# Copying the second half of the sums behind the third of four Silu passes in a fused decoder kernel

## What is computed

```python
q = (X @ W_Q + b_Q).reshape(Bv, Tv, H_TOT, DH).transpose(0, 2, 1, 3)   # 64 heads of 16
k = jnp.tile(k_base, (1, N_BR, 1, 1)); v = jnp.tile(v_base, (1, N_BR, 1, 1))
q, k = (_rope(q), _rope(k))
scores = jnp.einsum('bhtd,bhsd->bhts', q, k) * ATTNSCALE
w = jax.nn.softplus(scores / jnp.sqrt(key_self)[:, :, None, :])
w = jnp.where(causal, w, 0.0)
w = w * jax.nn.sigmoid(SCALE * w)                    # Silu, up to a factor
w = jnp.where(w < sinks, 0.0, w)                     # threshold
total = jnp.sum(w, axis=-1, keepdims=True) + sinks + 1e-06
out = jnp.einsum('bhts,bhsd->bhtd', w / total, v)    # the sums
out = out + probs_sink * v_null
y = jnp.einsum('bntc,ncd->bntd', context, W_O) + W_O_bias[None, :, None, :]
return y.mean(axis=1)
```

## Time and profile before

| | us |
|---|---|
| median of 3 runs | 3050.16 |
| lowest and highest run | 3041.3, 3050.38 |
| the profiled execution | 3048.71 |
| its span, first to last instruction | 3046.9 |
| PE busy in the span | 2660.8 (87%) |
| DVE busy | 1783.8 (59%) |
| ACT busy | 1558.1 (51%) |
| POOL busy | 801.1 (26%) |
| mean granted TensorE clock, share of full speed | 0.936 |

### The profile page before, as it was taken

The page is one execution under the profiler, slowest core; times in us unless marked ns, Lnnn a source line. Parts: engine busy times, 40 slices in busy tenths (PEclk is TensorE's granted clock), DMA queues, the critical chain, the costliest instruction groups (busy, mean ns, idle before and its releaser), DMA issues. The chain is left out here.

```text
span 3046.9 us, 49262 instructions
## 1 busy us (share of the span) xinstructions
PE 2660.8 (87%) x18536; PEld 2093.0 (69%) x18536; DVE 1783.8 (59%) x4040; ACT 1558.1 (51%) x3054; POOL 801.1 (26%) x889
## 2 busy tenths in 40 slices
PE   5888888888877689999979999999969999849998
PEld 4555555555545456777758888898967777748887
DVE  3565556546537656555646767666765555554444
ACT  2766566666545344444436656655546656542221
POOL 1222222222210144444432111111006666600000
PEclk8899899989879899999999999999989999979999
DMA  3000000000002211111110000000010000020000
GB/s 111 5 4 5 1 4 5 4 1 4 1 1 64 80 26 25 26 41 33 22 35 13 6 6 6 3 1 1 1 68 8 8 5 5 1 97 8 8 4 32
DMA packets 88763, 59.42 MB, mean 20 GB/s; under 512 B 55120, under 2 KB 78416, under 8 KB 88016
## 3 DMA queue, kind: packets, MB, share of 16 engines
q1 hardware_dynamic: 88528, 56.25, 6.2%
HBM read 39.46 MB, written 8.39 MB: 16 GB/s over the span
## 5 line engine op out<-in xcount | busy, mean ns | idle before, releaser
L682 DVE SCALAR_TENSOR_TENSOR a_w<-a_w,a_sinks 128x384 f32<-128x384 f32 x512 | 348.5, 734 | 79.2 <-ACT a_w L510 78.9
L2031 POOL TENSOR_SCALAR x_weights<-x_weights,x_sums 128x256 f32<-128x256 f32 x256 | 232.5, 928 | 272.4 <-DVE x_sums L2090 272.4
L1121 POOL TENSOR_SCALAR f_weights<-f_weights,f_sums 128x256 f32<-128x256 f32 x256 | 232.7, 928 | 271.2 <-DVE f_sums L1351 271.2
L491 ACT ACTIVATE a_w<-psum 128x1024 f32<-128x1024 f32 x192 | 187.2, 1029 | 207.6 <-PE psum L343 207.6
L338 PE MATMUL psum<-a_qT,a_kT_half 32*128 32x512 f32 x768 | 221.6, 658 | 6.9 <-ACT a_w L491 4.1
L1279 ACT ACTIVATE f_weights<-psum,f_negmax 128x256 f32<-128x256 f32 x256 | 118.0, 473 | 212.8 <-DVE f_negmax L1345 212.8
L343 PE MATMUL psum<-a_future,a_unit 32*128 32x128 f32 (+5 forms) x1536 | 218.2, 406 | 0.0
L1616 ACT ACTIVATE a_turned_w_hi<-psum 128x512 fp32r<-128x512 f32 x256 | 139.1, 596 | 142.5 <-PE psum L1526 142.5
L2001 ACT ACTIVATE x_weights<-x_masked_s,x_negmax 128x256 f32<-128x256 f32 x256 | 127.0, 497 | 137.2 <-DVE x_negmax L2082 137.2
L343 PEld LDWEIGHTS psum<-a_future,a_unit 32*128 32x128 f32 x1536 | 124.5, 197 | 97.8 <-issue 96.7
L1733 DVE TENSOR_REDUCE a_negmax<-psum 128x1 f32<-128x1024 f32 x128 | 156.6, 1224 | 55.7 <-PE psum L119 51.5
(11 more groups left out here) (357 smaller groups left out, 7395.7 us busy)
## 6 DMA issues: line engine op xcount, KB each, us to landing
f_xnT<-all_xnT_all SPq DMA_DIRECT2D x16, 256.0 KB, 2.3
f_pv_rows<-f_pv SPq DMA_DIRECT2D x8, 512.0 KB, 3.2
f_pv_groups<-f_pv_rows SPq DMA_DIRECT2D x8, 512.0 KB
f_w<-in_f_w SPq DMA_DIRECT2D x2, 2048.0 KB, 10.2
all_x_all<-in_x SPq DMA_DIRECT2D x1, 2048.0 KB, 8.5
a_xnT<-all_xnT_all SPq DMA_DIRECT2D x8, 256.0 KB, 2.3
x_xnT<-all_xnT_all SPq DMA_DIRECT2D x8, 256.0 KB, 2.3
x_ctxT<-in_x_ctxT SPq DMA_DIRECT2D x8, 256.0 KB, 2.9
```

The lines of the kernel that those rows point to most:

```text
L491: act.activation(to, of, ACT.Softplus).then_inc(plus_done, 1)
L682: ins = dve.scalar_tensor_tensor(part, part, sinks[:, col:col + 1], part, ALU.is_ge, ALU.mult)
L1121: ins = pool.tensor_scalar(w, w, sums[:, k, h, t:t + 1], None, ALU.mult)
L2031: ins = pool.tensor_scalar(w, w, sums[:, k, h, t:t + 1], None, ALU.mult)
```

## The change

In steps in which a quad has Silu passes, ACT's copy of the second half of the sums moves from behind the fourth Silu pass and the table loads (in step 4 also Ln and Exp) to a place between the third and the fourth Silu pass. In the steps without Silu passes the copy stays where it is. Its wait on `summed` and its signal `sums_taken` go with it.

```diff
@@ -508,6 +508,8 @@
                                     for h in range(2):
                                         wu = w[:, (2 * n + pair) % PAIR_RING, h].rearrange("p r t -> p (r t)")
                                         act.activation(wu, wu, ACT.Silu, scale=SILU_SCALE).then_inc(silu_done, 1)
+                                        if (pair, h) == (1, 0):
+                                            take_sums(sums_quad, 1, spare_bank(b, step, "sum", 1))
                             if ahead and step == 4:
 
                                 act.preload_act_table_set("natural_log_exp_and_others")
@@ -518,7 +520,8 @@
                                    .then_inc(knorm_ready, 1)
                             if quad or ahead and step == 4:
                                 act.preload_act_table_set("softplus")
-                            take_sums(sums_quad, 1, spare_bank(b, step, "sum", 1))
+                            if not quad:
+                                take_sums(sums_quad, 1, spare_bank(b, step, "sum", 1))
```

## The result

| | before | after | predicted |
|---|---|---|---|
| median, us | 3050.27 | 2974.01 | 2921 (2905 to 2960) |
| profiled execution, us (span) | 3048.71 (3046.9) | 2978.33 (2976.5) | |
| mean granted clock | 0.936 | 0.933 | |
| one full batch, us | 105.79 | 92.44 | 86.6 |

The ratio of after to before is 0.9754, 95% interval 0.9718 to 0.9791: faster by 2.5%, a little over half of what was forecast, and 14 us above the range. The direction and the cause of the stalls were right. The time that is missing went into TensorE's clock, at a place that the prediction named and took for unlikely.

What follows compares the result with a forecast made beforehand. TensorE was taken as the bound, stalled in even steps by ACT's late copy of the sums. Gains of 40.6 + 14.4 + 41.3 + 30.6 + 0.3 = 127.2 us took 3048.7 to 2921, range 2905 to 2960.

Steps and rivals of the forecast that it cites:

- What bounds the kernel, and why the copy came late: First self attention: TensorE sets the pace, idle 15.6 us a batch, waiting for ACT's copy behind four Silus and a load.
- No load for the copy: On ACT, the copy between Silus needs no table load; the rival with two loads, 2968, had 1 in 100.
- Step 0: Projections: stall shrinks by 2.7 us, 1.0 stays; full clock gains another 3.0; 5.8 a time, seven times, 40.6.
- Step 2: Window of step 2: the whole 2.40 us stall goes, no clock to be won; six times, 14.4.
- Step 4: Window of step 4: the 4.62 us stall goes, a new softplus stall of 1.4 appears; gain 5.9, seven times, 41.3.
- the new softplus stall lowers the clock: Rival, step 4: light work behind the new stall runs at half clock, losing up to 9.6 us; 2988, 5 in 100.
- Step 6: Output product: stall shrinks by 2.7 us, 2.0 stays; full clock gains another 2.4; 5.1 a time, six times, 30.6.
- the first rival: Clock still falls in the stalls left in steps 0 and 6; 35.4 us not won, 2957; 10 in 100.
- First and last batch: First batch: step 4's 5.9 us counted; last batch: step 0's 5.8 counted, its later steps nearly cancel, +0.3.
- The sum: Whole kernel: 40.6 + 14.4 + 41.3 + 30.6 + 0.3 = 127.2 us saved.
- The range: Whole kernel: 2906 to 2940 us for the forecast itself, 2905 to 2960 with most of the first rival.
- The second rival: Step 4: the new softplus stall lowers the clock, up to 9.6 us lost seven times, 67; 2988, 5 in 100.

Runs made afterwards that it cites:

- ln6_wait: Changed kernel with step 4's Ln, Exp and their load moved to step 6, plus two idle table loads ahead of step 4's softplus; 2966.5 us, ratio 0.9732.
- half2: Changed kernel with four more dense matmuls (0.86 us) in step 4's window, leaving part of the softplus wait; about 2961 us, ratio 0.9718.
- only4: Kernel before the change with the copy moved in step 4 alone, steps 0, 2 and 6 as before; 3053.3 us, ratio 1.0013.

## Why the prediction was wrong, by its own steps

- **What bounds the kernel, and why the copy came late.** Right. The stalls that it forecast, 1.0 in step 0, none in steps 2 and 4, 2.0 in step 6 and 1.4 for softplus, measured 0.93, none, 1.90 and 1.59 in the batch shown.
- **No load for the copy.** Right, as the earlier trace rows had it: the copy stands between the Silus with no load beside it. The Trainium skill's dearer switch with a drain ("ScalarE: Activation LUTs", "What ACT_TABLE_LOAD costs") is not to be seen after the change either: the fourth Silu ends at 380.92, the load starts at 380.94 and Ln at 382.23.
- **Step 0.** Right to 0.1 us, clock and DVE chain included: 2.9 + 2.8 against 5.8.
- **Step 2.** Right, 2.6 against 2.4.
- **Step 4.** The term itself is right, 5.9, and the next late wait was named. The step that failed is what it leaves behind: the prediction let the 20 us behind the new stall run at full clock and gave "the new softplus stall lowers the clock" 5 in 100. It happened in all seven batches (0.55 to 0.63 over the 14 us behind the wait), and cost 4.5 us in the batch shown. Its argument against was that dense projections come straight before; the changed kernel and ln6_wait show that they don't protect the stretch. A nearer row was on the table: the earlier trace rows hold a stall of 2.40 without a fall, but with projections behind it, and a stretch at 0.50 in the last batch, which stands behind a stall of the same length with light work behind it. The prediction reasoned from the first of these. PE in the kernel before, ahead of the stretch from 814.80:

```profile
812.47 0.66 PE L406 MATMUL psum<-all_ident,a_sumT 128*128 128x128 f32 x4 [2.40 <-ACT a_sumT L478]
813.38 1.13 PE L338 MATMUL psum<-a_qT,a_kT_half 32*128 32x512 f32 x4 [0.26 <-ACT a_w L491]
```

- **Step 6.** The stall was sized right (2.8 less against 2.7); the output product gained 0.8 instead of 2.4 in the batch shown. Here the first rival came true in part: 8.86 in most batches, and 7.07 in the one in which PE came too late to wait. In step 0 it did not: 1.00 behind the stall of 0.93.
- **First and last batch.** 5.9 and 6.1 were forecast, 0.4 each came. In the first, step 4's gain came, but 4.7 us were lost behind its new wait and as much behind the 1.0 wait of step 2, where the clock had held before the change: the first is the step that failed, the second is chance as far as these runs show. In the last, the clock was low from the first score slot behind step 2's window on (1.91 at 736.68), where before the change it held for that slot (1.13 at 813.38), and stayed at 0.51 for 44 us.
- **The sum.** 127 forecast, 70.4 in the profiled execution. Six full batches are short by some 7 us each, about 42, the first and the last by 11 together. The stages behind the first attention, which are the same code, took 3.8 us more in this one execution; why is open.
- **The range.** It reached to the first rival and not to the second, since each was given a chance of its own. They have one cause, a clock that falls behind short stalls, and should have been one case: with both, 3048.7 - (127 - 35 - 67) = 3024, and the measured 2974 lies between that and the forecast. The second rival's price was too high, up to 9.6 a batch against the 4.5 measured, because the clock came back within the stretch.

The Trainium skill's "TensorE: Matmul & The Clock Gate", section "A second HAM failure mode: psum-queue depth-cycling", says that frequent short idle times between matmul groups make the clock swing between half and full. The traces agree in so far as the clock falls behind waits of 0.77 us (run half2) to 1.64 us (changed kernel) and comes back. The Trainium skill says it there of a kernel that cycles through PSUM banks; here the wait was for softplus results, a few times a batch.

## What to carry to other kernels

Where a TensorE stall is removed, look for the next stall and for the work behind it, and price that work at half clock as well as at full. The price goes by the work: behind step 4's wait light work went on at half clock for some 10 us and lost 4.5; behind the 1.90 stall of step 6 the output product lost 1.8 (8.86 against 7.07). One row without a fall doesn't rule a fall out, as the 2.40 stall shows, with none in six batches of the kernel before and two in six of only4. A short wait that can't be removed may be filled with matmuls already at hand; here eight of them, 1.8 us of work done twice, made the changed kernel 43 us faster. And when the same stall has a fall behind it in some batches and none in others, the forecast is a spread between both prices, not one of them.

## What the runs showed of the hardware

- A TensorE wait of 0.77 us, in the same place of the same loop, was followed by the lower clock in four of six batches and not in the other two. Waits of 1.26 to 1.64 in step 4 of the changed kernel lowered it in seven of seven, to 0.55 to 0.63 over the 14 us behind them; waits of 1.14 to 1.52 in ln6_wait did in six of seven.
- In the changed kernel the clock came back under light work alone in the batch shown, after some 10 us in which PE was busy throughout (to about 399). In the last batch, with waits of 2.87 and 2.59 us among the light work, it stayed low: 40 us of 44 busy, 184 matmuls, granted 0.51.
- A TensorE wait of 1.0 us (0.99 to 1.01), in the same place of the first batch in all eleven traces, was followed by the lower clock in five (0.57 to 0.63 over the 14 us behind it) and by 1.00 in six.
- A stall of 2.40 us with projections behind it left the clock at full in six of six full batches of the kernel before and was followed by a fall in two of six of only4.
- Two table loads with no use between them run as written, and cost their 1.28 us each.
